# Swapped projections of the first item by TensorE, and orders changed around loads, items 28 to 30 and the second layer's MLP

## The reference, cut to what matters

```python
# layer 0: self attention, cross attention, MLP
attn_in = _adaln(x, cond, ln1_w, ln1_b, g1_w, g1_b, b1_w, b1_b)
x = _attn(attn_in, attn_in, sa_wq, sa_wkv, sa_wo, sa_bo) + x
cross_in = _adaln(x, cond, ...)
x = _attn(cross_in, _ln(context, ...), ca_wq, ca_wkv, ca_wo, ca_bo) + x
x = gelu(_adaln(x, cond, ...) @ ff_w1 + ff_b1) @ ff_w2 + ff_b2 + x

# in _attn: 16 heads of 64; q and k turned by sine and cosine of the position
xe, xo = x[..., ::2], x[..., 1::2]
re, ro = xe * c - xo * s, xe * s + xo * c
a = softmax(einsum(q, k) * 64 ** -0.5)
```

## Time and profile before

| | us |
|---|---|
| median of 3 runs | 415.65 |
| the three runs | 414.74, 415.65, 415.76 |
| the profiled execution | 415.27 |
| its span, first to last instruction | 412.9 |
| mean granted TensorE clock | 0.992 |

### The profile page before, as it was taken

One profiled execution on the slowest core, in us unless ns is written; L12 is line 12 of the kernel. 1 busy time (PEld: TensorE's weight loads), 2 busy tenths in 40 slices (PEclk: granted clock), 3 DMA queues, 4 the chain that ended last, 5 costly groups with the idle time before them and its releaser, 6 DMA issues. The chain is left out here.

```text
span 412.9 us, 9912 instructions
## 1 busy us (share of the span) xinstructions
PE 380.3 (92%) x3599; PEld 286.9 (69%) x3599; DVE 321.2 (78%) x696; ACT 298.5 (72%) x1033; POOL 155.7 (38%) x147
## 2 busy tenths in 40 slices
PE   7789998999999999999999897989899999999866
PEld 3547676777777777777777576776677787777554
...
DMA packets 15954, 26.08 MB, mean 63 GB/s; under 512 B 3582, under 2 KB 5892, under 8 KB 15780
## 3 DMA queue, kind: packets, MB, share of 16 engines
q1 hardware_dynamic: 13572, 18.49, 12.6%
...
q10 hardware_dynamic: 720, 1.00, 0.8%
...
HBM read 8.15 MB, written 0.52 MB: 21 GB/s over the span
## 5 line engine op out<-in xcount | busy, mean ns | idle before, releaser
L280 POOL TENSOR_TENSOR swp<-swp,small 128x512 f32<-128x512 f32 x64 | 81.9, 1293 | 123.1 <-PE bank L884 72.9
L406 ACT ACTIVATE prob<-bank,nmax 128x128 f32<-128x128 f32 x256 | 91.5, 391 | 5.0 <-DVE nmax L676 5.0
L501 ACT ACTIVATE raw<-bank,nmax 128x128 f32<-128x128 f32 x256 | 73.0, 393 | 13.1 <-DVE nmax L782 12.8
L406 ACT ACTIVATION_READ_ACCUMULATOR prob<-bank,nmax 128x1 f32 x256 | 59.3, 232 | 0.0
L782 DVE TENSOR_REDUCE nmax<-bank 128x4 f32<-128x512 f32 x64 | 41.2, 685 | 17.9 <-PE bank L884 17.8
L676 DVE TENSOR_REDUCE nmax<-bank 128x4 f32<-128x512 f32 x64 | 41.2, 685 | 17.1 <-PE bank L884 17.1
L683 DVE TENSOR_TENSOR prob<-prob,rz 128x512 f32<-128x512 f32 x64 | 50.3, 786 | 2.2
L884 PE MATMUL bank<-hT,wqkv 128*128 128x512 f32 x96 | 49.7, 603 | 1.1 <-ACT hT L389 1.1
L235 POOL TENSOR_TENSOR rstd<-vare,neg_half 128x4 f32<-128x4 f32 x12 | 12.4, 1033 | 96.3 <-DVE vare L611 96.1
L412 ACT ACTIVATE probT<-bank 128x512 f32<-128x512 f32 x32 | 19.1, 597 | 40.3 <-PE bank L970 40.3
L970 PEld LDWEIGHTS bank<-small,prob 128*128 128x128 f32 x256 | 28.6, 140 | 27.9 <-DVE prob L683 17.8
...
## 6 DMA issues: line engine op xcount, KB each, us to landing
swp<-raw SPq DMA_DIRECT2D x128, 128.0 KB, 2.1
...
```

The lines of the kernel that those rows point to most:

```text
L280: nc.gpsimd.tensor_tensor(four(swp[:, m % 2, f, :]), four(swp[:, m % 2, f, :]), sin[f], ALU.mult).then_inc(rope_sin[f], 1)
L406: last = nc.scalar.activation(prob[:, hh, bcols(u)], S[hh][:, bcols(u)], ACT.Exp, bias=nmax[:, s % 2, hh, u:u + 1], accum_out=zsum[:, s % ...
L501: last = nc.scalar.activation(prob1[:, s % 2, hh, bcols(u)], score_bank(s, hh)[:, bcols(u)], ACT.Exp, bias=nmax[:, s % 2, hh, u:u + 1])
```

## The change

- The swapped projections of item 0 are computed by TensorE (`fill_swapped`) from weight columns whose pairs are exchanged on the host (`wswap`, 128 KB, a new load on the sync queue); VectorE multiplies them by the sine (`first_rope`). Swap and sine of item 0 by DMA and GpSimd are gone. Projections of items 0 and 1 stand in `first_fills`; v of item 1 is projected in slot 0. Swaps and sines count from item 1, and the three small DMAs come after the swap of item 1.
- The context statistics go to slots 0 and 1 of VectorE, the aggregates to 1 and 2, GpSimd's part to 2 and 3.
- GpSimd: `loads(s)` goes ahead of the sines.
- VectorE: `shift0` goes ahead of the first `normalise` of a slot (it does something in slots 4, 13, 21 and 28). ScalarE's `scale_shift(2, 0, O)` goes ahead of slot 28's second exponentials.
- `normalise(29, 1)` goes to slot 29, ahead of the residual; in slot 30 `prob_values(29)` goes ahead of `transpose_norm(3, 0)`, and `ln_normalise(3, 0)` and the first sum of item 31 ahead of `normalise(30, 0)`.
- Layer 1: `turn_back(0)` and `divide(0)` go from slot 5 to slot 8, into bank Y, and `transpose_norm(3, 1)` no longer waits for them; ScalarE's `scale_shift(3, 1, Y)` goes ahead of slot 6's second exponentials.

The diff, cut to its core:

```diff
@@ -62,7 +62,12 @@
-def build(nc, small_in, x_in, ctx_in, ctxT_in, wqkv_in, wmod_in, wsq_in, wff_in, row_in, out):
+def swaps(m):
+    return (m + 1) // 2
+def build(nc, small_in, x_in, ctx_in, ctxT_in, wqkv_in, wswap_in, wmod_in, wsq_in, wff_in, row_in, out):
     es = ExitStack()
@@ -206,7 +212,7 @@
                 for f in range(2):
-                    sp.wait_ge(raw_out[f], m + 1)
+                    sp.wait_ge(raw_out[f], m)
                     if m >= 2:
@@ -214,13 +220,14 @@
             sp.dma_start(wqkv[:, 0, :], wqkv_in[:, 0, :]).then_inc(ld_wqkv[0], 16)
+            sp.dma_start(wswap[:, :], wswap_in).then_inc(ld_swap, 16)
             load_x(1)
             sp.dma_start(ctx[:, :, :], ctx_in.rearrange("b t d -> t b d")).then_inc(ld_ctx, 16)
-            swap(0)
+            swap(1)
             sp.wait_ge(row_part, 5)
...
                 sp.dma_start(parts_row[j:j + 1, :], parts[:, j, :]).then_inc(row_moved, 16)
-            for m in range(1, ITEMS):
+            for m in range(2, ITEMS):
                 swap(m)
@@ -276,7 +283,7 @@
             def rope_sine(m, f):
-                pool.wait_ge(swapped[f][m % 2], 32 * (m // 2 + 1))
+                pool.wait_ge(swapped[f][m % 2], 32 * swaps(m))
                 nc.gpsimd.tensor_tensor(four(swp[:, m % 2, f, :]), four(swp[:, m % 2, f, :]), sin[f], ALU.mult).then_inc(
@@ -313,15 +320,15 @@
                     pool.wait_ge(scores[0], s + 1)
-                if s + 1 < ITEMS - 1:
+                loads(s)
+                if 1 <= s + 1 < ITEMS - 1:
                     rope_sine(s + 1, 0)
                     rope_sine(s + 1, 1)
-                loads(s)
                 background0(s)
             def background0(s):
-                if s in (1, 2):
-                    context_inv_std(s - 1)
+                if s in (2, 3):
+                    context_inv_std(s - 2)
                 if s in (11, 19):
@@ -453,18 +460,17 @@
             def l0_slot(s):
-                if s < 0:
-                    evacuate_raw(s + 2, 0)
-                    evacuate_raw(s + 2, 1)
-                    evacuate_v(s + 2)
-                    return
                 if s >= 2:
...
                 exp0(s, 0)
+                if s == 0:
+                    evacuate_v(1)
                 if s + 2 < ITEMS:
                     evacuate_raw(s + 2, 0)
+                if s == 28:
+                    scale_shift(2, 0, O)
                 if s == 31:
@@ -490,8 +496,6 @@
                     scale_shift(1, s // RUN - 1, O)
-                if s == 28:
-                    scale_shift(2, 0, O)
                 if s == 30:
@@ -542,6 +546,8 @@
                     evacuate_o1(s // 4 - 1)
+                if s == 6:
+                    scale_shift(3, 1, Y)
                 if s < ITEMS and s != 5:
@@ -553,8 +559,8 @@
                         scale_shift(5, 1, Y)
-                if s in (3, 6):
-                    scale_shift(2 if s == 3 else 3, 1, Y)
+                if s == 3:
+                    scale_shift(2, 1, Y)
                 if s == 4:
@@ -579,7 +585,10 @@
             scale_shift(0, 0, T[0])
-            for s in range(-2, ITEMS):
+            evacuate_v(0)
+            evacuate_raw(1, 0)
+            evacuate_raw(1, 1)
+            for s in range(ITEMS):
                 l0_slot(s)
@@ -689,45 +698,55 @@
             def rope_cosine(m, f):
-                dve.wait_ge(raw_out[f], m + 1)
+                if m:
+                    dve.wait_ge(raw_out[f], m)
+                else:
+                    dve.wait_ge(filled[f], 1)
                 nc.vector.tensor_tensor(four(qk[:, m % 2, f, :]), four((X, Y)[f][:, :]), cos[f], ALU.mult).then_inc(
...
             def rope_sum(m, f):
-                dve.wait_ge(rope_sin[f], m + 1)
+                if m:
+                    dve.wait_ge(rope_sin[f], m)
+                else:
+                    dve.wait_ge(first_sin[f], 1)
                 dve.wait_ge(rope_cos[f], m + 1)
...
+            def first_rope(f):
+                dve.wait_ge(first_swap[f], 1)
+                nc.vector.tensor_tensor(four(swp[:, 0, f, :]), four(S[f][:, :]), sin[f], ALU.mult).then_inc(first_sin[f], 1)
+                rope_cosine(0, f)
+                rope_sum(0, f)
             def l0_slot(s):
-                if s >= 1:
+                if s >= 1 and s != 30:
                     normalise(s - 1, 1)
-                if s >= 0:
-                    row_max(s, 0)
-                    row_max(s, 1)
+                row_max(s, 0)
+                row_max(s, 1)
                 if s + 1 < ITEMS - 1:
...
                     copy_T0(s - 1)
-                if s >= 0:
-                    normalise(s, 0)
                 shift0(s)
+                if s == 30:
+                    ln_normalise(3, 0)
+                    rope_sum(31, 0)
+                normalise(s, 0)
                 if s + 1 < ITEMS:
-                    rope_sum(s + 1, 0)
+                    if s != 30:
+                        rope_sum(s + 1, 0)
                     rope_sum(s + 1, 1)
...
             def middle0(s):
-                if s == -1:
-                    context_stats(0)
-                    context_stats(1)
                 if s == 27:
                     ln_aggregate(2, 0)
-                if s == 30:
-                    ln_normalise(3, 0)
@@ -739,7 +758,9 @@
                 if s in (0, 1):
-                    context_aggregate(s)
+                    context_stats(s)
+                if s in (1, 2):
+                    context_aggregate(s - 1)
                 if s in (2, 3):
@@ -764,6 +785,7 @@
                     rope_cosine(ITEMS - 1, 1)
+                    normalise(29, 1)
                     residual(2, 0, O, acc_done[0], 1)
@@ -789,10 +811,9 @@
                 dve.wait_ge(back, g + 1)
-                bank = Y if g else W
-                src = bank[:, :].rearrange("p (i u h v) -> p i u h v", i=4, u=HALF, h=2)
+                src = Y[:, :].rearrange("p (i u h v) -> p i u h v", i=4, u=HALF, h=2)
                 recip = rzo[:, :].rearrange("p (i u h) -> p i u h", i=4, u=HALF)
-                nc.vector.reciprocal(rzo[:, :], bank[:, :].rearrange("p (r v) -> p r v", v=VW // 2)[:, :, DH1]).then_inc(
+                nc.vector.reciprocal(rzo[:, :], Y[:, :].rearrange("p (r v) -> p r v", v=VW // 2)[:, :, DH1]).then_inc(
                     rzo_done, 1)
@@ -829,6 +850,8 @@
                     ln_normalise(3, 1)
+                if s == RUN:
+                    divide(0)
                 for run in range(RUNS):
@@ -854,8 +877,6 @@
                     scale_shift_last(2 if s == 3 else 3, 1, W)
-                if s == 5:
-                    divide(0)
@@ -871,8 +892,10 @@
             dve.wait_ge(ld_tab, 16)
-            rope_cosine(0, 0)
-            for s in range(-1, ITEMS):
+            first_rope(1)
+            first_rope(0)
+            rope_cosine(1, 0)
+            for s in range(ITEMS):
                 l0_slot(s)
@@ -1011,7 +1034,7 @@
                 if half:
-                    pe.wait_ge(proj_out, AT["q", 1] + 1)
+                    pe.wait_ge(o_norm, 1)
                 else:
@@ -1058,21 +1081,40 @@
+            def fill_swapped(f):
+                mm(S[f][:, :], wswap[:, f * P:(f + 1) * P], hT[:, 0, :], True, True).then_inc(first_swap[f], 1)
+            def first_fills():
+                wait_hT(0, 0)
+                pe.wait_ge(ld_wqkv[0], 16)
+                pe.wait_ge(ld_swap, 16)
+                fill_swapped(1)
+                fill(0, 1)
+                fill_swapped(0)
+                fill(0, 0)
+                fill(0, 2)
+                fill(1, 0)
+                fill(1, 1)
             def l0_slot(s):
-                if s < 0:
-                    for f in range(3):
-                        fill(s + 2, f)
-                    return
                 score(s)
+                if s == 0:
+                    fill(1, 2)
                 if s >= 1:
...
                     project_out(s - 2)
+                if s == 30:
+                    prob_values(29)
                 if s != 29:
                     background0(s)
-                if s + 2 < ITEMS:
+                if s == 0:
+                    fill(2, 1)
+                    fill(2, 2)
+                elif s + 2 < ITEMS:
                     fill(s + 2, 2)
@@ -1081,7 +1123,7 @@
                     project_values(0)
-                if s >= 30:
+                if s == 31:
                     prob_values(s - 1)
@@ -1179,7 +1221,7 @@
                 if g == 0:
-                    pe.wait_ge(gelu_done, FF + 2)
+                    pe.wait_ge(proj_out, AT["q", 1] + 1)
                 elif g == 1:
@@ -1187,7 +1229,7 @@
                 for i in range(4):
-                    last = nc.tensor.transpose((Y if g else W)[:, bcols(i)], oS[:, bcols(i)], ident)
+                    last = nc.tensor.transpose(Y[:, bcols(i)], oS[:, bcols(i)], ident)
                 last.then_inc(back, 1)
@@ -1224,6 +1266,8 @@
                     project("k", 1)
+                if s == RUN:
```

(7 more changed lines are left out.)

15 lines of the change are left out of this document (9 added, 6 removed).

## The result

The changed kernel takes 412.52 us (median of 5 runs, 411.34 to 412.55), where the kernel before took 415.65 in runs taken with it (414.3 to 416.62, 5 runs). The ratio of after to before is 0.9937, with a 95% interval of 0.9913 to 0.9961. So it is faster, by 3.1 us of medians. The forecast was 408.9 with a range of 406.2 to 411.9: the time lies 3.6 above the forecast and 0.6 above the range. Of the 6.8 us that the sum promised, less than half came.

A forecast was written before the change was run, and what follows sets the result against it. TensorE, busy 92% of a 412.9 us span, was taken as the bound. Terms 2.1 + 0.7 + 1.1 + 0.8 + 2.1 = 6.8 off 415.27 gave 408.5, with 0.4 for the median 408.9; range 406.2 to 411.9.

The forecast's parts named there:

- part 1: Opening, first item: swapped projections computed on TensorE bring scores of item 1 2.1 us earlier, with 1.2 given back.
- the first term: Opening: scores of item 1 start at 23.3 instead of 25.42, 2.1 us earlier (ends 1.1 and 2.8).
- the 1.2 "given back": Slots 0 to 2: context statistics and aggregates moved there, with nothing covering them, lose 1.2 us (ends 0.6 and 1.6).
- Rival A: Opening and layer 1: TensorE's low clock comes back after gaps, price 1.5 us, total 410.4; chance 0.18.
- Rival B: Opening gives back all it gains; slots 3 and 5 keep late sines; terms -2.3, total 411.2; chance 0.18.
- part 2: Slots 0 to 13: weight loads issued ahead of GpSimd's sines land before the next swap, so fewer sines are late.
- 0.45 for slot 3 and 0.75 for slot 5: Layer 0: earlier sines let slot 3's normalisation end sooner and slot 5's sums and next scores come on time.
- 0.7 for slots 13 and 14: Layer 0: earlier 1 MB load removes a 0.53 wait; earlier scale-and-shift brings 0.2; together 0.7 us (0 to 1.1).
- my -0.4 and +0.4 for slots 8 to 11: Layer 0, slots 8 to 11: a gain of 0.4 us and a loss of 0.4 us from loads ahead of the sines.
- rival E: Delayed sines hold the port lock past TensorE's slack at each slot; full price 9.3 us, total 418.2; chance 0.03.
- part 3: Items 28 to 31: reordering removes waits, 1.1 us in slot 28 and 0.8 from slot 30's waits.
- part 4: Layer 1, slots 5 to 9: turn-back moved to slot 8 removes its wait and low clock, 2.1 us (1.0 to 2.6).

The follow-up runs named there:

- before_again: The kernel before, rerun with no edit: 414.87 us, ratio 1.0002.
- a_again: The changed kernel, rerun with no edit: 412.48 us, ratio 0.9931.
- a_loads_behind: The changed kernel with GpSimd's weight loads put back behind the sines in every slot: 413.07 us, ratio 0.9943.
- a_ff_split: The changed kernel with the 1 MB MLP weight load cut into four of 256 KB, behind the sines of slots 13 to 16: 412.07 us, ratio 0.9936.
- a_warm: The changed kernel with dummy matmuls of zeros in TensorE's gaps of the opening and the last MLP: 410.77 us, ratio 0.9881.
- b_loads: The kernel before with only the weight loads moved ahead of the sines: 414.24 us, ratio 1.0.
- b_items_layer1: The kernel before with only the new orders of items 28 to 31 and layer 1, and shift0 ahead of the normalisation: 412.84 us, ratio 0.9947.
- a_ctx_early: The changed kernel with the context statistics moved from slots 0 and 1 into VectorE's waits of the opening: 410.82 us, ratio 0.9884.
- b_but_opening: The kernel before with every part of the change except the opening: 411.33 us, ratio 0.9942.

## Why the prediction was wrong

Each part of the sum, beside what the profile of after gained on it against the two profiles of the kernel before:

| stretch | forecast | against before | against before_again |
|---|---|---|---|
| opening, to item 3 | 0.9 | -0.34 | -0.27 |
| slots 3 to 12 | 1.2 | 0.35 | 0.49 |
| slots 13 and 14 | 0.7 | 1.10 | 0.57 |
| slots 15 to 27 | none | -0.58 | -0.59 |
| slots 28 to 30 | 1.9 | 1.84 | 1.54 |
| layer 1, items 5 to 9 | 2.1 | 1.77 | 0.85 |
| last MLP and end | none | -1.7 | -1.7 |
| sum of the span | 6.8 | 2.4 | 0.8 |

Stretches that aren't listed differ by under 0.1 in all. So three terms were too large (opening, loads, layer 1), and two stretches without a term lost time.

**The opening, part 1: two terms too good.** The first scores came at 16.82 (16.4 was forecast) at full clock, and the swapped fills, their readable times and VectorE's six operations of 0.7 came as worked out: the sums end at 15.6, 15.3 was forecast. 0.17 of the difference is a first hT that was later (10.05 against 9.88 in the earlier trace rows). Item 1 came at 24.24, not 23.3: 0.4 of that was there at item 0, and the rest is the landing of the swap's second part, used at 21.99, where I had taken 21.2. That is the late end of the two that I gave. So the first term is 1.18 in place of 2.1, which is 0.92 of the 1.24 that the opening lacks; the other 0.32 is the 1.2 "given back". I took the context work at its own length less VectorE's slack. It cost TensorE more: between items 1 and 3 after takes 16.07 and before 14.55, so 1.52 was given back; with the statistics placed early the same stretch takes 14.32. So the statistics behind the q cosine cost 1.75 from item 1 to item 3, waits and half clock together. Rival A's mechanism was in the prediction, and it happened: 1.2 GHz came in all four profiled openings of this kind that left a gap behind item 1's scores (after, a_again, a_loads_behind, and a_ff_split at 24.4), and in none with the statistics early or with dummies. Its price is in a_warm: 0.36 by item 3, not 1.5, as VectorE's queue is the limit there. Rival B, the opening that gives all back, is what came: it had the swap at 22 (21.99), the context work at 1.6 (1.52) and terms that leave slots 0 to 11 at -0.2 in place of 2.1, where the profiles show 0.26 at item 12. It was given 0.18. What it didn't name is the way, a wait of TensorE's with half clock behind it, and its 411.2 is still 1.3 below the measured time.

**The loads, part 2: the mechanism came, the gain didn't.** I took 0.45 for slot 3 and 0.75 for slot 5, and 0.7 for slots 13 and 14. The sines are mostly in time, as forecast. But slot 3's sines start 2.64 behind the scores in after and 2.79 before. I had them 1.4 behind the scores, forgetting that the two loads in front take 1.2: there the delay by issue replaces the delay by landing. Slot 5 took 7.09 in after where it had 7.46, which is half of my 0.75, and 7.48 in a_again. Over slots 3 to 12 the loads ahead bring 0.11 by b_loads against before_again and lose 0.18 by after against a_loads_behind: zero. The step that failed is the pricing slot by slot by the sines of one profile: which sines are late, and by how much, isn't the same in the next. What stays is the delay in slots 11 and 12, which take 6.78 or 6.79 and 7.06 with loads ahead and 6.64 or 6.65 and 6.80 or 6.81 with loads behind, in every profile; my -0.4 and +0.4 for slots 8 to 11 allowed for that, slot 12 had no term. In after:

```profile
103.06 2.52 POOL L287 TENSOR_TENSOR swp<-swp,small 128x512 f32<-128x512 f32 x2
105.03 1.10 DVE L692 TENSOR_TENSOR prob<-prob,rz 128x512 f32<-128x512 f32 x1
109.30 0.66 PE L993 MATMUL bank<-small,prob 128*128 128x128 f32 x4 [0.34 <-DVE prob L692]
```

The normalisation of slot 11 takes 1.10 beside the later sines, 0.69 before, and the one behind it comes late for TensorE in slot 12. That is the mechanism of rival E, the lock. The profile of after shows its sign: the first normalisation takes 1.10 to 1.40 in seven of slots 0 to 11, where before has three over 1. But it cost 0.4 in slots 11 and 12 together and nothing like its price of 9.3: the earlier trace rows and the slack of 0.4 decided rightly.

Slots 13 and 14 came out better than forecast, 1.10 for 0.7, and neither part of it comes from the load's place. 0.74 is slot 14, where a late sine of before is missing from before_again and b_loads too (6.65 and 6.64). 0.36 is slot 13, where another edit acts: the wait for the scale and shift is 0.85 before, 1.07 in before_again and b_loads, 0.40 in after and 0.39 in b_items_layer1, which has `shift0` first and the loads behind. This I had put at 0.2 and it is 0.45 to 0.67. Slots 13 and 14 were longest with a late swap beside the 1 MB load, on either side of the sines: ahead of them 9.54 in slot 13 of a_again, behind them 8.27 in slot 14 of b_items_layer1.

The Trainium skill says in DMA: Bandwidth & Descriptors, "Issuing engines are not separate DMA queues", that transfers of all issuers run on the same 16 DMA engines and interleave. The 3.88 of wait behind the 1 MB load in a_again agrees with it. Why one execution of the same order has it and another hasn't isn't settled (see what stays open).

**Items 28 to 31, part 3: right.** Forecast 1.1 and 0.8, sum 1.9. Measured 1.08 in slot 28 (12.42 to 11.34) and 0.76 in slots 29 and 30 (18.51 to 17.75), sum 1.84; against before_again 0.93 and 0.61. As forecast, no wait for the scale and shift is left in slot 28, and new small waits have taken the place of the old ones. TensorE in after:

```profile
246.49 1.09 PE L907 MATMUL bank<-probT,v 128*64 128x128 f32 x16 [0.50 <-DVE x L608]
...
250.65 1.09 PE L907 MATMUL bank<-probT,v 128*64 128x128 f32 x16 [0.49 <-DVE probT L698]
252.58 0.66 PE L993 MATMUL bank<-small,prob 128*128 128x128 f32 x4 [0.24 <-DVE prob L692]
```

The first of these waits was there before, only 0.07 shorter:

```profile
247.95 1.09 PE L884 MATMUL bank<-probT,v 128*64 128x128 f32 x16 [0.43 <-DVE x L599]
```

So normalisation 29 ahead of the residual, which I had set at zero, costs 0.07 at most, although it takes 1.66 in after beside GpSimd's sine (0.69 in five other profiles with this order). Slot 29 is 0.16 longer in after and as long as before in four others; slots 28 and 29 together take 23.16 to 23.27 in all eleven profiles with the new order and 24.01 to 24.35 in the three with the old. Slot 30 takes 5.85 to 5.87 and 6.62 to 6.77.

**Layer 1, part 4: the mechanism was right, the term was mis-sized.** Forecast 2.1. The profile of before minus that of after gives 20.79 - 19.02 = 1.77, which looks like a near hit. But against before_again and b_loads it is 0.85 and 0.87. The other 0.9 is the stretch at 0.62 of the earlier trace rows, which I had charged to the gap of 1.17 and counted as removed. It was there in one of three profiles of this code, though the gap was the same: 1.17 in the earlier trace rows, 1.18 in before_again. TensorE in after:

```profile
290.36 0.67 PE L907 MATMUL bank<-swp,vst 128*32 128x128 f32 x16 [0.18 <-DVE swp L809]
...
292.64 0.66 PE L918 MATMUL bank<-small,xn 128*128 128x128 f32 x4 [0.60 <-POOL xn L249]
...
299.16 0.66 PE L1232 MATMUL bank<-small,oS 128*128 128x128 f32 x4
```

The waits are as rebuilt (0.18 for 0.3, 0.60 for 0.6, none at the moved turn-back), and the scores of slot 8 come at 298.07 on a scale 2.36 earlier, 300.4 on the old one, for 300.2. So the rebuilding was good to 0.2; what was wrong was the starting point.

**What no step had.** The last MLP ran 1.7 slower in after, with the same gaps in front of it as in the kernel before. 1.2 GHz stood there in four of the seven profiles with the new layer 1 and no dummies (after, a_loads_behind, a_ctx_early, b_items_layer1), and in none of three with the old one. The sum had no term for it, and dummies in those gaps give the 1.7 back (a_warm). Since half clock appears at one place or another in nearly every execution, the prediction should have counted a chance stretch as it stands, neither gone nor new. The other stretch without a term is slots 15 to 27, which take 94.3 to 94.4 in all five profiles with the old opening and 94.7 to 96.3 in all nine with the new one. b_but_opening and after differ by the opening alone, and take 94.3 and 94.9. So the new opening costs about 0.6 there as well, far behind the edit.

**The sum again**, without luck of the clock in layer 1, as an estimate from the profiles: opening -0.4 (item 3, the four new against the five old), slots 15 to 27 -0.5, loads 0, slots 13 and 14 about 0.5, items 28 to 31 1.7, layer 1 0.85, about 2.2, against 2.6 by the ratio (1.6 to 3.6) and 3.1 of medians.

**What stays open.** Why swaps land late with no load in flight: in after the k sines of items 18 and 20 (at 148.01 and 163.49) wait 1.04 and 0.82 for their landing, and slots 18 to 20 take 22.06 where 21.47 stood before; in the four kernels with dummies slot 24 takes 7.07 to 7.26 where all others show 6.65. The traces point at instruction fetches (queue q8 of the page, 16 KB each). In slots 16 to 27 of the fourteen profiles a fetch begins 0.1 to 1.1 behind the start of the scores 20 times, and in 18 of these slots the k sine starts 1.7 to 3.2 behind the q sine; in the other 148 slots it is 1.5 at most. All 20 are in kernels with the new opening. In slot 13 such a fetch stands at 0.54 in a_again and 0.45 in a_ctx_early, the two with the long slot, and none in after; but a_warm has one at 0.34 and no long slot. No run moved the fetches alone, so this is a correlation and not a shown cause. Whether the new timing makes the half clock in the last MLP more frequent isn't settled either. And by the times alone the opening can't be given a sign; by the starts it loses.
